# First layer of two tiles in four blocks as seven block products, with planned engine lists

## The chip, the cores and the metric

The kernel runs on one core of one Trainium2 chip. The metric is the device time of one execution in microseconds; before the change the median of three runs is 625.27 us.

## The reference

Input x is 4 x 512 tokens of 256 features. It goes through a gated attention-like layer and then a feed-forward stack, each with a layer normalization before and after and a residual. The change is in the stack, six blocks of:

```python
for i in range(N_BLOCKS):                      # 6
    h = gelu(einsum('bsd,hd->bsh', x, W1[i]) + B1[i])      # 256 -> 1024
    x = einsum('bsh,dh->bsd', h, W2[i]) + B2[i] + x        # 1024 -> 256
    if i < N_BLOCKS - 1:
        x = layernorm(x, LN_G[i], LN_B[i])                 # over the 256 features
```

## The kernel before, in words

A **tile** is one batch of 512 tokens; n = 4 * block + tile numbers the 24 passes of the stack. Features lie on partitions (two chunks k of 128), tokens on the free axis. Every number is held as a high part (fp32r) and a low remainder: XH/XL for activations, WH/WL for weights, HH/HL for the hidden layer. A product of two such numbers is three matmuls (low by high, high by low, high by high), issued by `mm3` (L161 to L167).

A **unit** (n, j) is 128 of the 1024 hidden features of one tile. `mm1` (L326) computes it in 6 matmuls of 512 columns (two chunks of features, three matmuls each) into one of four PSUM banks. ScalarE takes two Gelus from it: `ghi` (L970) writes the high part HH, `gf` (L979) the full value back to PSUM; VectorE's `hlo` (L564) subtracts them to HL. `mm2` (L340) multiplies the unit with the second layer, again 6 matmuls, into the tile's two accumulation banks. From block 1 on TensorE alternates mm1 and mm2, three units apart (L400 to L402, bank order `STEADY`).

After a tile's eight units VectorE adds bias and residual (`y`, L572), and normalizes over partitions: GpSimd adds the chunks (`sum1`, L1249), VectorE transposes and reduces (`tr1`, `red1`), the result goes to DRAM (`put1`, L1343) and comes back to all partitions in four transfers (`got1`, L1347), VectorE totals (`tot1`) and spreads it by a transpose (`mub`), and centres (`ctr`). The same again for the squares: `sqr` (ScalarE), `sum2` (GpSimd), `tr2`, `red2`, `put2`, `got2`, `tot2`, `vae`, then `rsd` (GpSimd, L1259, a power of -0.5), `rsb` and `nn` (L637). `xhi` (ScalarE, L993) and `xlo` (VectorE, L645) split the result for the next block.

Weights of a block come in four pieces p through a staging buffer STG of two halves (`ldp`, L1334), are rounded by ScalarE (`wp_hi`, L843) and their remainder is taken by GpSimd (`wp_lo`, L1169). `kv` (L514) belongs to the attention part.

Each engine works through a list in order. For the attention part and blocks 0 to early 1 the lists are written out call by call (L378 to L399, L712 to L748, L1047 to L1076, L1285 to L1296, L1399 to L1425); then loops follow (L400, L749, L1077, L1297, L1426); the last block's end is written out again. Between engines there are only semaphores, so an instruction late on one engine holds all behind it in that list.

## Time and profile before

| | |
|---|---|
| median of 3 runs | 625.27 us (625.22 to 625.55) |
| the profiled execution | 625.31 us, its span 623.5 us |
| TensorE, VectorE, ScalarE, GpSimd busy | 99%, 74%, 66%, 40% of the span |
| TensorE's mean granted clock | 0.998 of full speed |
| DMA | 25.13 MB moved, mean 40 GB/s |

The profile comes from one execution. Busy time is the union of an engine's instructions, which can overlap on one engine; "idle before, releaser" is what ended the wait ahead of an instruction. L numbers are lines of the kernel before.

### The profile page before, as it was taken

The page shows a single profiled execution, that of the slowest core. Times are in us where ns is not written, and L with a number is a line of the kernel's source. Part 1 is how long each engine was busy: PE and PEld are TensorE (multiplying, and loading weights), DVE is VectorE, ACT ScalarE, POOL GpSimd, SP SyncE. Part 2 cuts the span into 40 slices and gives each one's busy share as a digit, 9 for nine tenths or more (in the row PEclk, how much of TensorE's full clock was granted, in tenths as well). Part 3 has the DMA queues.
Part 4 walks back from the last instruction along what each step waited for, and adds up shares of the span by engine and source line. Part 5 has one row for each costly group of instructions (what it writes and reads, how often), then busy time and mean ns, then how long its engine had stood idle before and what let it go on. Part 6 is the DMA issues. An engine that isn't in the chain of part 4 may idle for free.

```text
span 623.5 us, 8868 instructions
## 1 busy us (share of the span) xinstructions
PE 617.3 (99%) x2893; PEld 516.5 (83%) x2893; DVE 459.9 (74%) x826; ACT 409.0 (66%) x688; POOL 248.7 (40%) x233
## 2 busy tenths in 40 slices
PE   9999999999999999999999999999999999999996
PEld 7888888888888888888888888888888888888886
DVE  6999758886677778676787667767766867666676
ACT  6999986778756675566566556755656665555554
POOL 6666501537434353334532253442344422301234
PEclk9999999999999999999999999999999999999999
DMA  7210000003111020101200110200111100003544
GB/s 293 69 35 1 2 2 0 4 1 106 36 39 40 7 68 6 37 6 37 58 20 3 39 39 2 72 6 5 37 39 38 38 4 6 5 3 68 94 91 156
DMA packets 55821, 25.13 MB, mean 40 GB/s; under 512 B 46816, under 2 KB 51808, under 8 KB 55776
## 3 DMA queue, kind: packets, MB, share of 16 engines
q1 hardware_dynamic: 53376, 24.05, 15.2%
q10 hardware_dynamic: 2400, 0.52, 0.4%
q8 instruction: 23, 0.38, 0.3%
q14 instruction: 22, 0.18, 0.1%
HBM read 20.03 MB, written 4.52 MB: 39 GB/s over the span
## 4 chain that ended last, share of the span: by engine, by line
PE 95%; DVE 1%; DMA 1%; POOL 1%; ACT 0%; issue 0%; ACTq 0%; SPq 0%
PE BK L166 47%; PE BK L356 40%; PE BK L306 4%; PE BK L267 1%; PE BK L270 1%; PE BK L268 1%; PE BK L240 1%; PE BK L260 0%; PE BK L252 0%; PE BK L251 0%; DMA X<-in_x 0%; PE BK L230 0%; DVE R L709 0%; DMA turns<-TB 0%; DMA R<-turns 0%; DVE ST L675 0%
## 5 line engine op out<-in xcount | busy, mean ns | idle before, releaser
L976 ACT ACTIVATE HH<-BK,SM 128x512 fp32r<-128x512 f32 x192 | 132.1, 689 | 153.3 <-PE BK L166 148.3
L569 DVE TENSOR_TENSOR HL<-BK,HH 128x512 fp32r<-128x512 f32 x192 | 131.2, 685 | 84.0 <-ACT BK L982 82.0
L166 PE MATMUL BK<-XH,WL 128*128 128x512 f32 x416 | 162.4, 390 | 0.0
L166 PE MATMUL BK<-XL,WH 128*128 128x512 f32 x416 | 162.1, 390 | 0.0
L166 PE MATMUL BK<-XH,WH 128*128 128x512 f32 x416 | 162.0, 389 | 0.0
L356 PE MATMUL BK<-HH,WL 128*128 128x512 f32 x368 | 143.5, 390 | 0.0
L356 PE MATMUL BK<-HH,WH 128*128 128x512 f32 x368 | 143.2, 389 | 0.0
L356 PE MATMUL BK<-HL,WH 128*128 128x512 f32 x368 | 143.2, 389 | 0.0
L982 ACT ACTIVATE BK<-BK,SM 128x512 f32<-128x512 f32 x192 | 125.2, 655 | 0.0
L166 PEld LDWEIGHTS BK<-XH,WL 128*128 128x128 f32 x416 | 78.1, 188 | 16.6 <-DVE MS L551 0.3
L166 PEld LDWEIGHTS BK<-XH,WH 128*128 128x128 f32 x416 | 78.1, 188 | 16.3
L166 PEld LDWEIGHTS BK<-XL,WH 128*128 128x128 f32 x416 | 78.1, 188 | 15.8
L1263 POOL TENSOR_TENSOR RN<-VN,MH 128x16 f32<-128x16 f32 x20 | 58.7, 2935 | 62.4 <-DVE VN L628 62.4
L356 PEld LDWEIGHTS BK<-HL,WH 128*128 128x128 f32 x368 | 69.1, 188 | 14.3
L356 PEld LDWEIGHTS BK<-HH,WH 128*128 128x128 f32 x368 | 69.1, 188 | 14.3
L356 PEld LDWEIGHTS BK<-HH,WL 128*128 128x128 f32 x368 | 69.1, 188 | 14.2
L1177 POOL TENSOR_TENSOR WL<-STG,WH 128x512 fp32r<-128x512 f32 x48 | 64.5, 1361 | 36.7 <-ACT WH L850 36.6
L1257 POOL TENSOR_TENSOR SA<-SA,TB 128x512 f32<-128x512 f32 x20 | 25.9, 1293 | 127.3 <-ACT TB L991 127.3
L1253 POOL TENSOR_TENSOR SA<-R 128x512 f32<-128x512 f32 x20 | 25.9, 1293 | 39.6 <-DVE R L577 39.6
L1001 ACT ACTIVATE XH<-R,SM 128x512 fp32r<-128x512 f32 x40 | 27.7, 724 | 19.6 <-DVE R L642 19.6
L577 DVE SCALAR_TENSOR_TENSOR R<-BK,SM,R 128x512 f32<-128x512 f32 x46 | 33.5, 731 | 3.4 <-PE BK L356 3.4
L642 DVE SCALAR_TENSOR_TENSOR R<-R,SM,MB 128x512 f32<-128x512 f32 x40 | 35.5, 922 | 0.5
(165 smaller groups left out, 790.1 us busy)
## 6 DMA issues: line engine op xcount, KB each, us to landing
STG<-in_w SPq DMA_DIRECT2D x24, 512.0 KB, 3.8
G<-sums SPq DMA_DIRECT2D x160, 8.0 KB, 1.7
out<-R SPq DMA_DIRECT2D x16, 128.0 KB, 2.0
X<-in_x SPq DMA_DIRECT2D x3, 512.0 KB, 7.7
R<-turns SPq DMA_DIRECT2D x3, 512.0 KB, 4.1
turns<-SA SPq DMA_DIRECT2D x12, 64.0 KB, 2.0
sums<-P SPq DMA_DIRECT2D x40, 8.0 KB, 1.4
R<-in_wv SPq DMA_DIRECT2D x1, 512.0 KB, 5.4
```

The costliest lines, as they stand in the source:

```text
L166: r = eng.matmul(dst, s, m, start=i == 0, stop=i == len(todo) - 1)
L356: r = eng.matmul(acc_of(n)[k][:, :], w, h[:, hs, :], start=(j == 0 and i == 0), stop=(j == 7 and i == 2))
L569: eng.tensor_tensor(HL[:, g % HR, :], bank["mm1", n, j][:, :], HH[:, g % HR, :].bitcast(f32), ALU.subtract).then_inc(S["hlo"], 1)
L577: eng.scalar_tensor_tensor(feat(t, k), by_chunk(acc_of(n)[k][:, :]), BS[:, 2 * b + k:2 * b + k + 1], feat(t, k), ALU.add, ALU.add).then_in ...
L642: eng.scalar_tensor_tensor(feat(t, k), feat(t, k), LG[:, 2 * b + k:2 * b + k + 1], by_chunk(MB[:, 1, :]), ALU.mult, ALU.mult).then_inc(S[" ...
L976: eng.activation(HH[:, g % HR, :], bank["mm1", n, j][:, :], ACT.Gelu, bias=B1[:, 8 * (n // 4) + j:8 * (n // 4) + j + 1]).then_inc(S["ghi"], 1)
L982: eng.activation(ps[:, :], ps[:, :], ACT.Gelu, bias=B1[:, 8 * (n // 4) + j:8 * (n // 4) + j + 1]).then_inc(S["gf"], 1)
L1001: eng.activation(by_chunk(XH[:, F_SLOT[t], k, :]), feat(t, k), ACT.Identity, bias=LB[:, 2 * b + k:2 * b + k + 1]).then_inc(S["xhi"], 1)
L1177: eng.tensor_tensor(WL[:, b % 2, a:a + 512], STG[:, p % 2, 512 * h:512 * h + 512], WH[:, b % 2, a:a + 512].bitcast(f32), ALU.subtract).the ...
L1253: eng.tensor_tensor(by_chunk(SA[:, :]), feat(n % 4, 0), feat(n % 4, 1), ALU.add).then_inc(S["sum1"], 1)
L1257: eng.tensor_tensor(SA[:, :], SA[:, :], TB[:, :], ALU.add).then_inc(S["sum2"], 1)
L1263: eng.tensor_tensor(RN[:, :], VN[:, :], MH[:, :], ALU.pow).then_inc(S["rsd"], 1)
```

## The change

In blocks 1 to 4 (`PAIRED`) tiles 0 and 1 go through the first layer together. The weight (1024 x 256) and the activations of the pair (256 x two tiles) are taken as two-by-two blocks, and the four block results come from seven block products (Strassen's scheme in the form with four sums on each side) in place of eight. Per quarter q of 128 features in each half of the hidden layer there are seven products of three matmuls (`prod1` to `prod7`), for the units (4b, q), (4b, q+4), (4b+1, q), (4b+1, q+4). Two results are copied by ScalarE (`bcopy`, PSUM to PSUM; `tcopy`, PSUM to KB) and added by VectorE (`dsum`, `esum`). The four sums of weights are made by GpSimd (`sadd`, remainder `slo`; ScalarE `shi`), those of activations by VectorE (`tsum`, remainder `tlo`; ScalarE `thi`); three activation blocks are used as they are (`bhi`, `blo`, in place of `xhi`, `xlo`). The second layer is as before. The sums of the normalization are fetched by one transfer instead of four, and may be one tile further ahead. The lists of all engines from block 0's end to block 4 are written out anew, by a planner in which a VectorE instruction and a GpSimd instruction may lock each other out. Some semaphores are merged. Attention and block 5 stay. The core of the diff:

```diff
+PAIRED = (1, 2, 3, 4)
...
+def paired(n):
+    return n // 4 in PAIRED and n % 4 < 2
+
+
+def place(n, j):
+    if not paired(n):
+        return 8 * n + j
+    return 32 * (n // 4) + 4 * (j % 4) + ((1, 2) if n % 4 == 0 else (0, 3))[j // 4]
...
+        def s_weights(i, q):
+            return ((UH, OH)[i // 2][:, i % 2, 128 * q:128 * q + 128], (UL, OL)[i // 2][:, i % 2, 128 * q:128 * q + 128])
...
+            def product(dst, s, m, first, last):
+                for i, (w, v) in enumerate(((s[1], m[0]), (s[0], m[1]), (s[0], m[0]))):
+                    r = eng.matmul(dst[:, :], w, v, start=first and i == 0, stop=last and i == 2, skip_group_check=True)
+                return r
+
+            def prod1(b, q, a, c, d, e):
+                claim(a)
+                pe.wait_ge(S["plo"], 7 * (b - 1) + 3)
+                pe.wait_ge(S["wp_lo"], 8 * b + 4)
+                bank["pair", b, q] = BK[a], BK[c], BK[d], BK[e]
+                bank["before", b, q] = freed[c], freed[d], freed[e]
+                for x, (n, j) in ((a, (4 * b + 1, q)), (d, (4 * b, q)), (e, (4 * b, q + 4)), (c, (4 * b + 1, q + 4))):
+                    bank["mm1", n, j] = BK[x]
+                    freed[x] = S["hlo"], place(n, j) + 1
+                product(BK[a], w_ffn(b, 128 * q, 128), home(B11), True, True).then_inc(S["prod"], 1)
+
+            def prod2(b, q):
+                pe.wait_ge(S["plo"], 7 * (b - 1) + 6)
+                pe.wait_ge(S["pcopy"], 8 * (b - 1) + 2 * q + 1)
+                product(bank["pair", b, q][0], w_ffn(b, 1024 + 128 * q, 128), home(B21), False, True).then_inc(S["mm1"], 1)
+
+            def prod3(b, q):
+                pe.wait_ge(S["plo"], 7 * (b - 1) + 1)
+                pe.wait_ge(S["slo"], 4 * b)
+                pe.wait_ge(S["padd"], 8 * (b - 1) + 2 * q + 1)
+                product(bank["pair", b, q][2], s_weights(3, q), home(B22), False, True).then_inc(S["mm1"], 1)
+
+            def prod4(b, q):
+                pe.wait_ge(S["plo"], 7 * b)
+                pe.wait_ge(S["padd"], 8 * (b - 1) + 2 * q + 2)
+                product(bank["pair", b, q][1], w_ffn(b, 1536 + 128 * q, 128), t_home(b, 3), False, True).then_inc(S["mm1"], 1)
+
+            def prod5(b, q):
+                before = bank["before", b, q][2]
+                pe.wait_ge(*before)
+                pe.wait_ge(S["plo"], 7 * (b - 1) + 4)
+                pe.wait_ge(S["slo"], 4 * b - 3)
+                product(bank["pair", b, q][3], s_weights(0, q), t_home(b, 1), True, True).then_inc(S["prod"], 1)
+
+            def prod6(b, q):
+                pe.wait_ge(S["plo"], 7 * (b - 1) + 5)
+                pe.wait_ge(S["slo"], 4 * b - 2)
+                pe.wait_ge(S["pcopy"], 8 * (b - 1) + 2 * q + 1)
+                product(bank["pair", b, q][1], s_weights(1, q), t_home(b, 2), False, True).then_inc(S["prod"], 1)
+
+            def prod7(b, q):
+                pe.wait_ge(S["plo"], 7 * (b - 1) + 2)
+                pe.wait_ge(S["slo"], 4 * b - 1)
+                pe.wait_ge(S["padd"], 8 * (b - 1) + 2 * q + 1)
+                product(bank["pair", b, q][1], s_weights(2, q), t_home(b, 0), False, True).then_inc(S["mm1"], 1)
...
-            for g in range(8 * 4, 8 * (4 * NB - 1)):
-                mm1(g // 8, g % 8, STEADY[g % 4])
-                mm2((g - LAG) // 8, (g - LAG) % 8)
+            for b in range(1, NB):
+                if b in PAIRED:
+                    a, e, c, d = STEADY
+                    for q in range(4):
+                        g = 32 * b + 4 * q
+                        mm2(*unit(g - 3))
+                        prod1(b, q, a, c, d, e)
+                        prod5(b, q)
+                        mm2(*unit(g - 2))
+                        prod2(b, q)
+                        prod6(b, q)
+                        mm2(*unit(g - 1))
+                        prod3(b, q)
+                        prod7(b, q)
+                        mm2(*unit(g))
+                        prod4(b, q)
+                        e, c, d = d, e, c
+                first_g = 32 * b + (16 if b in PAIRED else 0)
+                for g in range(first_g, min(32 * b + 32, 8 * (4 * NB - 1))):
+                    mm1(*unit(g), STEADY[g % 4])
+                    if b not in PAIRED or g > first_g + 2:
+                        mm2(*unit(g - LAG))
+                    elif g == first_g:
+                        for back in (3, 2, 1):
+                            mm2(*unit(g - back))
...
+            def tsum(b, i):
+                n, p = 4 * b - 4, 2 * (b - 1)
...
+                else:
...
+                ve.wait_ge(S["nn"], 2 * n + (2, 3, 3, 4)[i])
...
+                dst, bias = by_chunk(QB[:, i, :]), LB[:, p + 1:p + 2]
+                if i == 0:
...
+                    r = eng.scalar_tensor_tensor(dst, feat(0, 1), DL[:, b - 1:b], feat(0, 0), ALU.add, ALU.subtract)
+                elif i == 1:
+                    r = eng.tensor_tensor(dst, feat(0, 0), feat(1, 0), ALU.subtract)
+                elif i == 2:
+                    r = eng.scalar_tensor_tensor(dst, feat(0, 1), bias, by_chunk(QB[:, 1, :]), ALU.add, ALU.subtract)
+                else:
+                    r = eng.scalar_tensor_tensor(dst, feat(1, 1), bias, by_chunk(QB[:, 2, :]), ALU.add, ALU.subtract)
+                r.then_inc(S["tsum"], 1)
...
+            def blo(b, i):
+                t, k = ((0, 1), (1, 0), (1, 1))[i]
+                hi, lo = b_home(i)
+                ve.wait_ge(S["phi"], 7 * (b - 1) + (1, 3, 6)[i])
+                eng.scalar_tensor_tensor(by_chunk(lo), feat(t, k), LB[:, 2 * (b - 1) + k:2 * (b - 1) + k + 1],
+                                         by_chunk(hi.bitcast(f32)), ALU.add, ALU.subtract).then_inc(S["plo"], 1)
+
+            def tlo(b, i):
+                hi, lo = t_home(b, i)
+                ve.wait_ge(S["phi"], 7 * (b - 1) + (2, 4, 5, 7)[i])
+                eng.tensor_tensor(lo, QB[:, i, :], hi.bitcast(f32), ALU.subtract).then_inc(S["plo"], 1)
+
+            def dsum(b, q):
+                _, c, d, _ = bank["pair", b, q]
+                ve.wait_ge(S["prod"], 12 * (b - 1) + 3 * q + 3)
+                ve.wait_ge(S["pcopy"], 8 * (b - 1) + 2 * q + 2)
+                ve.wait_ge(*bank["before", b, q][1])
+                eng.tensor_tensor(d[:, :], c[:, :], KB[:, q % 2, :], ALU.add).then_inc(S["padd"], 1)
+
+            def esum(b, q):
+                _, c, _, e = bank["pair", b, q]
+                ve.wait_ge(S["mm1"], place(4 * b, q + 4) + 1)
+                ve.wait_ge(S["pcopy"], 8 * (b - 1) + 2 * q + 2)
+                eng.tensor_tensor(e[:, :], c[:, :], KB[:, q % 2, :], ALU.add).then_inc(S["padd"], 1)
...
+            nn(1, 0); tr1(2); hlo(3, 4); tsum(1, 1); blo(1, 1); hlo(3, 5); tlo(1, 1); tsum(1, 2); hlo(3, 6)
+            nn(1, 1); hlo(3, 7); tlo(1, 2); blo(1, 2); tsum(1, 3); red1(2); tlo(1, 3); dsum(1, 0); hlo(5, 0)
...
+            tr2(8); red2(8); hlo(11, 0); tr2(9); red2(9); hlo(11, 1); tot2(8); vae(8); hlo(11, 2); y(10, 0)
+            y(10, 1); rsb(8); tot2(9); nn(8, 0); hlo(11, 3); vae(9); nn(8, 1); tr1(10); tsum(3, 0); hlo(11, 4)
+            blo(3, 0); tlo(3, 0); rsb(9); hlo(11, 5); nn(9, 0); nn(9, 1); tsum(3, 1); blo(3, 1); hlo(11, 6)
+            tsum(3, 2); tlo(3, 1); tsum(3, 3); hlo(11, 7); tlo(3, 2); blo(3, 2); tlo(3, 3); red1(10); dsum(3, 0)
+            hlo(13, 0); y(11, 0); y(11, 1); tot1(10); esum(3, 0); mub(10); hlo(12, 0); ctr(10, 0); hlo(12, 4)
+            ctr(10, 1); hlo(13, 4); tr2(10); dsum(3, 1); red2(10); hlo(13, 1); tr1(11); esum(3, 1); hlo(12, 1)
...
+            def bhi(b, i):
+                t, k = ((0, 1), (1, 0), (1, 1))[i]
...
+                eng.activation(by_chunk(b_home(i)[0]), feat(t, k), ACT.Identity,
+                               bias=LB[:, 2 * (b - 1) + k:2 * (b - 1) + k + 1]).then_inc(S["phi"], 1)
+
+            def thi(b, i):
+                ac.wait_ge(S["tsum"], 4 * (b - 1) + i + 1)
...
+                eng.activation(t_home(b, i)[0], QB[:, i, :], ACT.Copy).then_inc(S["phi"], 1)
+
+            def shi(b, h):
+                ac.wait_ge(S["sadd"], 4 * (b - 1) + 2 * h + 2)
...
+                eng.activation((UH, OH)[h][:, :, :], SB[:, 2 * h:2 * h + 2, :], ACT.Copy).then_inc(S["shi"], 1)
+
+            def bcopy(b, q):
+                a, c, _, _ = bank["pair", b, q]
+                ac.wait_ge(S["prod"], 12 * (b - 1) + 3 * q + 1)
+                ac.wait_ge(*bank["before", b, q][0])
+                eng.activation(c[:, :], a[:, :], ACT.Copy).then_inc(S["pcopy"], 1)
+
+            def tcopy(b, q):
+                i = 4 * (b - 1) + q
+                ac.wait_ge(S["prod"], 3 * i + 2)
+                if i > 1:
+                    ac.wait_ge(S["padd"], 2 * i - 2)
...
+                eng.activation(KB[:, q % 2, :], bank["pair", b, q][3][:, :], ACT.Copy).then_inc(S["pcopy"], 1)
...
+            gf(11, 3); ghi(11, 4); gf(11, 4); bhi(3, 0); thi(3, 0); ghi(11, 5); gf(11, 5); ghi(11, 6); bhi(3, 1)
+            gf(11, 6); thi(3, 1); ghi(11, 7); gf(11, 7); thi(3, 2); bhi(3, 2); thi(3, 3); bcopy(3, 0); tcopy(3, 0)
+            ghi(13, 0); gf(13, 0); wp_hi(17); ghi(12, 0); gf(12, 0); wp_hi(18); ghi(12, 4); gf(12, 4); ghi(13, 4)
...
+            def dl():
...
+                eng.tensor_tensor(DL[:, :], pairs[:, 1, :], pairs[:, 0, :], ALU.subtract).then_inc(S["bias"], 1)
...
+            def sadd(b, i):
...
+                a11, a21 = STG[:, 1, 0:512], STG[:, 1, 512:1024]
+                a12, a22 = STG[:, 0, 0:512], STG[:, 0, 512:1024]
...
+                left, right, op = ((a21, a22, ALU.add), (SB[:, 0, :], a11, ALU.subtract), (a11, a21, ALU.subtract),
+                                   (a12, SB[:, 1, :], ALU.subtract))[i]
+                eng.tensor_tensor(SB[:, i, :], left, right, op).then_inc(S["sadd"], 1)
+
+            def slo(b, i):
+                hi, lo = (UH, OH)[i // 2], (UL, OL)[i // 2]
+                po.wait_ge(S["shi"], 2 * (b - 1) + i // 2 + 1)
+                eng.tensor_tensor(lo[:, i % 2, :], SB[:, i, :], hi[:, i % 2, :].bitcast(f32),
+                                  ALU.subtract).then_inc(S["slo"], 1)
...
+            wp_lo(5, 0); l3_ve(3); l3_ng(3); l3_rs(3); sadd(1, 0); l3_nb(3); sadd(1, 1); rsd(0); slo(1, 0); sum2(1)
+            slo(1, 1); sadd(1, 2); sadd(1, 3); wp_lo(5, 1); slo(1, 2); slo(1, 3); wp_lo(6, 0); wp_lo(6, 1); rsd(1)
+            sum1(2); wp_lo(7, 0); wp_lo(7, 1); wp_lo(8, 0); wp_lo(8, 1); sadd(2, 0); sadd(2, 1); sadd(2, 2)
...
+                if b in PAIRED and i > 1:
+                    sp.wait_ge(S["sadd"], 4 * (b - 1) + i + 1)
...
-                eng.dma_start(SUMS[n, 0], P1[:, n % 2, :]).then_inc(S["put1"], 16)
+                eng.dma_start(SUMS[n, 0].rearrange("q (g b) -> g q b", g=4), P1[:, n % 2, :]).then_inc(S["put1"], 16)
...
-                for h in range(4):
-                    eng.dma_start(G1[32 * h:32 * h + 32, n % 2],
-                                  SUMS[n, 0].rearrange("(g q) b -> q g b", g=4)).then_inc(S["got1"], 16)
...
+                eng.dma_start(G1[:, n % 2].rearrange("p g b -> p (g b)"),
+                              SUMS[n, 0].unsqueeze(0).to_broadcast([4, 32, 64])).then_inc(S[f"got1_{n % 2}"], 16)
...
```

## Rows read from the trace of the kernel before

**Rows 1.** The page's busy times, share of the span and instruction count

```profile
PE 617.3 (99%) x2893; PEld 516.5 (83%) x2893; DVE 459.9 (74%) x826; ACT 409.0 (66%) x688; POOL 248.7 (40%) x233
```

**Rows 2.** All waits of TensorE: who for whom, us, times, longest

```profile
PE BK L172 <- POOL IDLE L1111: 0.9, 1, 0.9
PE BK L196 <- DVE R L449: 0.3, 1, 0.3
PE BK L267 <- DVE UL L489: 0.2, 1, 0.2
```

**Rows 3.** Stretches: window, length, busy (count) of PE PEld DVE ACT POOL

```profile
287.00:374.00 87.00, 87.00 (x386) 72.06 (x385) 63.35 (x101) 53.06 (x85) 32.99 (x20) 1.00 0.12 29
```

**Rows 4.** Timeline of TensorE: start, length, instruction; 87 rows between these

```profile
350.19 0.39 PE L166 MATMUL BK<-XL,WH 128*128 128x512 f32 x1
...
370.13 0.39 PE L166 MATMUL BK<-XH,WH 128*128 128x512 f32 x1
```

**Rows 5.** Groups by line: shape, count, busy us, mean ns, idle before

```profile
L982 ACT ACTIVATE BK<-BK,SM 128x512 f32<-128x512 f32 x192 | 125.2, 655 | 0.0
L1177 POOL TENSOR_TENSOR WL<-STG,WH 128x512 fp32r<-128x512 f32 x48 | 64.5, 1361 | 36.7 <-ACT WH L850 36.6
L1263 POOL TENSOR_TENSOR RN<-VN,MH 128x16 f32<-128x16 f32 x20 | 58.7, 2935 | 62.4 <-DVE VN L628 62.4
L648 DVE SCALAR_TENSOR_TENSOR XL<-R,SM,XH 128x512 fp32r<-128x512 f32 x40 | 33.2, 863 | 3.6 <-ACT XH L1001 3.5
L1001 ACT ACTIVATE XH<-R,SM 128x512 fp32r<-128x512 f32 x40 | 27.7, 724 | 19.6 <-DVE R L642 19.6
L850 ACT ACTIVATE WH<-STG 128x1024 fp32r<-128x1024 f32 x24 | 25.5, 1061 | 4.2 <-DMA STG<-in_w 2.5 <-PE BK L356 1.7
L521 DVE SCALAR_TENSOR_TENSOR BK<-KB,BK 128x512 f32<-128x512 f32 x8 | 5.5, 691 | 2.0 <-ACT KB L942 1.3 <-PE BK L166 0.7
```

**Rows 6.** Timeline of VectorE, three instructions with no wait between

```profile
362.81 0.67 DVE L616 TENSOR_REDUCE P<-TB 128x16 f32<-128x512 f32 x1
363.40 0.74 DVE L577 SCALAR_TENSOR_TENSOR R<-BK,SM,R 128x512 f32<-128x512 f32 x1
364.06 0.68 DVE L569 TENSOR_TENSOR HL<-BK,HH 128x512 fp32r<-128x512 f32 x1
```

**Rows 7.** Timelines of VectorE and SP: one round trip through DRAM

```profile
234.80 0.68 DVE L616 TENSOR_REDUCE P<-TB 128x16 f32<-128x512 f32 x1
...
239.98 0.26 DVE L622 TENSOR_REDUCE VS<-G 128x16 f32<-128x64 f32 x1 [0.41 <-DMA G<-sums]
...
235.50 0.34 SPq L1357 DMA_DIRECT2D sums<-P  x1
236.92 1.75 SPq L1364 DMA_DIRECT2D G<-sums  x4
```

**Rows 8.** Timelines of TensorE, ScalarE, VectorE: a unit from matmul to hlo

```profile
351.09 0.39 PE L166 MATMUL BK<-XH,WH 128*128 128x512 f32 x1
...
351.52 0.69 ACT L976 ACTIVATE HH<-BK,SM 128x512 fp32r<-128x512 f32 x1 [1.48 <-PE BK L166]
...
352.79 0.69 DVE L569 TENSOR_TENSOR HL<-BK,HH 128x512 fp32r<-128x512 f32 x1
```

**Rows 9.** Timelines of TensorE and VectorE where block 1 begins

```profile
178.60 0.39 PE L166 MATMUL BK<-XH,WL 128*128 128x512 f32 x1
...
184.25 1.82 DVE L642 SCALAR_TENSOR_TENSOR R<-R,SM,MB 128x512 f32<-128x512 f32 x1
```

**Rows 10.** Stretches with written-out lists, columns as in rows 3; sum of 20:178

```profile
20.00:40.00 20.00, 20.00 (x120) 17.48 (x119) 19.83 (x41) 18.87 (x35) 12.07 (x13) 1.00 0.17 54
...
sum 158.00, PE 158.00 PEld 134.52 DVE 126.57 ACT 128.37 POOL 75.61; mean PE 79.00 PEld 67.26 DVE 63.28 ACT 64.18 POOL 37.80
```

**Rows 11.** Timelines of VectorE and GpSimd: two xlo alone, two beside wp_lo

```profile
353.43 1.42 DVE L648 SCALAR_TENSOR_TENSOR XL<-R,SM,XH 128x512 fp32r<-128x512 f32 x2
...
376.14 2.97 DVE L648 SCALAR_TENSOR_TENSOR XL<-R,SM,XH 128x512 fp32r<-128x512 f32 x2 [0.90 <-ACT XH L1001]
...
375.57 2.98 POOL L1177 TENSOR_TENSOR WL<-STG,WH 128x512 fp32r<-128x512 f32 x2 [4.03 <-ACT WH L850]
```

516 lines of the change are left out of this document (318 added, 198 removed).

## The prediction

> **What bounds the kernel now.** I read the shares of the page first: TensorE is busy 99% of the span, VectorE 74%, ScalarE 66%, GpSimd 40% [rows 1]. Then the waits of TensorE: three in the whole execution, 1.4 us together [rows 2]. Then the table by stretches: in a full block of four tiles (the row stands for four alike) TensorE is busy 87.00 of 87.00 us at full clock (2.4 GHz), VectorE 63, ScalarE 53, GpSimd 33 [rows 3]. So time falls only if TensorE gets fewer columns to stream, and it rises only if TensorE is made to wait. The pace is read from its timeline: 88 matmuls between the starts at 350.19 and 370.13, 0.2266 us each, although one lasts 0.39 [rows 4]. A block has 32 units of 12, 384 matmuls, and 384 x 0.2266 is the 87.0.
>
> **What is removed.** For tiles 0 and 1 of blocks 1 to 4 the first layer was 16 units of 6 matmuls (96). Now each of four quarters runs seven products of 3 matmuls (21 for 24), so 84: 12 fewer per block, 48 in all. 48 x 0.2266 = 10.9 us. The second layer keeps its 6 per unit. All of it lies on the path, as TensorE has no idle time to absorb it. The execution whose rows I use took 625.31 us (span 623.5), 0.04 over the median of the three runs, 625.27; I work against 625.31. With no new stall: 625.3 - 10.9 = 614.4.
>
> The Trainium skill ("TensorE: Matmul & The Clock Gate", Back-to-back issue gap) gives N/2.4 + 2.5 ns for isolated matmuls, 216 ns at 512 columns; by it the 48 would be worth 10.4 us. The rows say 227 ns, and decide.
>
> **What is added, per block.** *ScalarE:* 4 thi, 3 bhi for 4 xhi, 2 shi of twice the width, 8 copies out of and into PSUM. With 0.66 to 0.72 us for a 512-wide activation and 1.06 for the wide one [rows 5] that is about 15 x 0.66 + 2 x 1.06 - 0.72 = 11 us of busy time: 53 becomes 64 of a block that now takes 84.3 (372 x 0.2266), 76%. Hidden by TensorE; if uncovered it would cost where a Gelu is late, but a Gelu pair takes 1.24 us and TensorE wants one per some 2.5 us.
> *VectorE:* 4 tsum, 4 tlo, 3 blo for 4 xlo, 4 dsum, 4 esum. At 0.69 to 0.86, and most near the lower [rows 5], about 15 x 0.72 = 11 us: 63 becomes 74 of 84.3, 88%. Back to back, though, these instructions start 0.59 to 0.66 us apart while each shows about 0.7 [rows 6], and "busy" already counts the overlap once, so 72 to 74 is the load.
> *GpSimd:* 4 sadd and 4 slo at 1.36, the same shape as wp_lo [rows 5], 10.9 us: 33 becomes 44, 52%.
> *DMA:* each total of the normalization was fetched by four transfers, now by one. Before: red2 starts 234.80 and lasts 0.68, tot2 starts 239.98 after waiting for the transfer; the put is issued at 235.50, the four gets at 236.92 and take 1.75 us to issue, against 0.34 for one transfer [rows 7]. One get should save about 1.75 - 0.34 = 1.4: from 4.5 to 3.1 us. On no path today; it buys slack for the chain below. SP's list changes order with it; its waits on sadd and wp_lo stand ahead of puts, but none that I can find waits longer than one or two GpSimd instructions.
> The renamed semaphores and the dl instruction cost nothing: they hide among GpSimd's idle time; uncovered, dl would be one short instruction of 0.2 us.
>
> **The new joints in a quarter.** TensorE's order, in matmuls: mm2 (0-6), prod1, prod5 (-12), mm2 (-18), prod2, prod6 (-24), mm2 (-30), prod3, prod7 (-36), mm2 (-42), prod4 (-45), so 10.2 us a quarter. A consumer starts about 0.2 us after the last matmul's slot: the unit starting at 351.09 is used at 351.52, and after both Gelus its hlo starts at 352.79, 1.27 later [rows 8]. bcopy has 12 matmuls (2.7 us) and needs 0.2 + 0.66. dsum must lie between the end of prod6 and prod3: 6 matmuls, 1.36 us, against 0.2 + 0.69 (its nearest row is kv, PSUM and SBUF in, PSUM out, 0.69 [rows 5]) + 0.1. Slack 0.37 us, if VectorE is free at that moment. The same for esum, between prod7 and prod4. These 32 sums are the tight joints: a VectorE instruction just begun costs up to 0.3 us. hlo of the unit wanted at once (mm2(g)) has 15 matmuls, 3.4 us, for 0.2 + 1.24 + 0.6 and a dsum: 0.7 or more over.
>
> **The new boundary.** The tiles of a pair end together, and both must be normalized, split and combined before the next block. I count from the end of the second tile's last mm2. TensorE then has 15 units of mm1 and 14 of mm2 before prod1, 29 x 6 = 174 matmuls, 39.4 us; prod5 needs its data at 40.1, prod2 at 42.2. VectorE in that stretch, from esum to the next dsum (231 matmuls, 52.4 us): 60 instructions of 512 columns and 6 short ones, 60 x 0.65 to 60 x 0.73 plus 1.3, 40 to 45 us. It fits. The chain of one tile alone, by its steps: y 1.3, sum1 1.3, transpose and reduction 1.3, DMA 3.1, total and spread 0.9, centring 1.3, squares 1.3, sum2 1.3, transpose and reduction 1.3, DMA 3.1, total 0.5, rsd 2.94 [rows 5], rsb 0.7: 20 us. The two tiles take turns in it, and the lists hold it back further. vae of the second tile stands behind the hlo of unit 3 of tile 3; that unit's mm1 ends at 4.08 + 8 x 2.72 = 25.8, so the hlo can't start before 27.3. So vae about 29, rsd 32, rsb (behind five instructions for the first tile) 33.8, then nn, tsum, blo, tlo packed tight: blo for prod1 at 37.2 (2.2 us early), tlo for prod5 at 39.1 (1.0 early), blo for prod2 at 41.8 (0.4 early). So it is just in time. The first boundary is alike: block 1's first matmul starts at 178.60 today while tile 1's nn runs at 184.25 [rows 9]; it must move up by over 5 us, with eight more GpSimd instructions (10.9 us) ahead of rsd(1), and the hlo of unit 4 of tile 3 queued behind tr1(2), which waits for sum1 behind that rsd. I count 0 to 2 us there.
>
> **What the joints cost.** No trace row has a dsum. Lower end: nothing, and no gain beyond the 48 matmuls, as the clock is at its top. For it speaks the stretch whose lists are already written out instruction by instruction: from 20 to 178 us TensorE is busy 158.00 of 158.00 while VectorE is at 80%, in one stretch of 20 us even at 19.83 [rows 10]. Upper end: 0.15 us at each of 16 quarters and 1 us at each of four boundaries, 6.4 us. I take 0.2 at each boundary and 0.05 at each quarter, 1.6 us, near the low end because the written-out stretch is the nearest row. **Forecast: 614.4 + 1.6 = 616.0.**
>
> **VectorE against GpSimd.** Two xlo take 1.42 us where GpSimd is idle and 2.97 where it runs two wp_lo, which themselves take 2.98 against a mean of 1.36 each [rows 5, 11]: 1.55 us lost for VectorE. An hlo, with one input in PSUM, shows nothing of the kind. tsum 1, tlo and the others with two SBUF inputs are of the first sort, dsum and esum of the second, but they queue behind it. The Trainium skill ("SBUF — State Buffer", Who interferes with whom) calls this an exclusive lock for the whole instruction, taken by whoever starts first, for VectorE instructions with two SBUF inputs; by it, 8 more GpSimd instructions a block speak against the change. The trace agrees, with the 2.97. In the new lists the last stretch before prod1 has no GpSimd work (wp_lo waits for a wp_hi that ScalarE has behind bcopy), so I charge it only in the rivals.
>
> **Rivals.**
> *Boundaries late.* An rsd, or slo ahead of sum1, slips by one locked instruction (1.3 to 1.55 us) on a chain with 0.4 to 1.0 us of slack: about 1.1 us per boundary, 4.4, plus 0.1 at each quarter, 1.6: 614.4 + 6.0 = 620.4. For it: the packed end. Against: the shorter DMA.
> *Slower: locked VectorE at the sums.* At each dsum and esum VectorE is in an instruction stretched by 0.78 us (half of the 1.55); less 0.37 of slack that is 0.41, and 32 x 0.41 = 13 us: 627.5. It decides from 0.34 us of stall per sum (10.9 / 32). Against: only a few of the 32 follow a two-SBUF-input instruction with GpSimd at work.
> *A draw.* Sums late by 0.3 each: 9.6 us, 624.0 and up. The same holds if the matmuls saved only let TensorE reach waits on other engines earlier, that is if the change takes matmuls away but not time. Against: VectorE at 88%, not 100.
>
> **How the numbers follow.** Forecast 0.70, boundaries late 0.20, draw 0.04, slower 0.06. A measurement tells 0.2% (1.25 us) from nothing, so faster is below 624.0: 0.90; same 0.04; slower 0.06. The range runs from 614.2 (no stall, less a little scatter) to 621.0 (6.4 us of joints, and the first rival); beyond lie the other two.
>
> **What would show it.** Right: 48 fewer matmuls, the rest 0.2266 apart; TensorE's waits for VectorE's dsum and esum small; VectorE 72 to 75 us a block; a paired quarter 10.2 us; red to tot near 3.1 us. Wrong: TensorE waits of over 0.3 us at prod3 or prod4 in most quarters, one of 1 us and more at prod1, prod5 or prod2 of a block, or a granted clock that falls.

## The result and the profile after

The changed kernel takes **631.31 us** (median of 4 runs, 629.07 to 632.11) beside 625.31 for the kernel before: the ratio is 1.0091, 95% interval 1.0078 to 1.0103. Forecast were 616.0 and a range up to 621.0. The profiled execution took 631.38. The first lines of its page; L numbers from here on are lines of the changed kernel:

```profile
span 629.5 us, 8835 instructions
...
PE 614.7 (98%) x2845; PEld 506.2 (80%) x2845; DVE 502.3 (80%) x886; ACT 439.1 (70%) x740; POOL 298.6 (47%) x266
...
PE 73%; DVE 12%; DMA 6%; issue 4%; ACT 3%; POOL 1%; SPq 1%; ACTq 0%; DVEq 0%; POOLq 0%
```

Against [rows 1]: 48 matmuls fewer, as said, yet TensorE is busy only 2.6 us less, and the chain of the end now runs through VectorE (12%) and transfers (6%). Block 2 in two stretches, the quarters of products first (columns as in rows 3):

```profile
273.00:316.60 43.60, 41.36 (x176) 32.05 (x174) 35.57 (x54) 30.57 (x50) 21.04 (x13) 1.00 0.17 52
316.60:361.50 44.90, 44.90 (x199) 37.17 (x198) 37.17 (x61) 30.31 (x50) 23.96 (x15) 1.00 0.02 4
```

Together VectorE is busy 72.7 us of 88.5 (forecast 72 to 75), and the second stretch is without a gap. So the loads were right; the waits were not. Those of TensorE and of the totals, and of the queue of transfers (who for whom: us, times, longest; [rows 2] had 1.4 us in all for TensorE):

```profile
DVE MU L731 <- DMA G<-sums: 16.3, 12, 3.7
...
DVE VS L759 <- DMA G<-sums: 7.4, 8, 2.9
...
PE BK L403 <- DVE BK L830: 2.8, 4, 1.2
...
PE BK L302 <- DVE HL L706: 2.1, 1, 2.1
...
PE BK L403 <- DVE BK L836: 2.0, 2, 1.7
...
SPq L1671 <- POOL WL L1480: 76.5, 17, 11.5
```

L830 is dsum, L836 esum, L403 a product, L302 a transpose of the attention's output; L731 and L759 are the totals tot1 and tot2, L1671 is ldp. In the kernel before the totals waited 5.8 and 8.8 us for their transfers, and ldp 23.7 us, four times.

**Where the 17 us went.** Two landmarks on TensorE's timeline: the start of the first product of block 1, and the length of each block's stretch from the start of its first product to the start of the matmul behind its last (174 matmuls). Undisturbed, the first product starts at 178.60 [rows 9] plus six matmuls, 179.96; a stretch takes 174 x 0.2267 = 39.44. The 198 matmuls between two stretches took 44.87 to 44.90 us for 44.88 at all three places: nothing is lost there, and prod1, prod5 and prod2 of blocks 2 to 4 wait for nothing. All is lost before the first product (5.3 us, a clock fall in it) and inside the stretches (3.4, 4.2, 3.0, 1.1). The sum is 17.0, and 631.4 - 614.4 = 17.0. The same for the kernels of this study (from the last product to the end are 140.1 to 140.2 us more; in e1_sp, e3_start, e4_nosum, g1_start and h1_spstart 140.7 to 141.0, with 0.55 to 0.61 of the excess behind TensorE's last matmul, the cause open; f2_old loses another 0.5 between blocks 1 and 2). The landmarks are those of the one profiled execution, which took 633.35 us in e2_tot, 630.96 in f3_start and 627.83 in i1_lists, so differences of under 1 us in one landmark prove little by themselves:

| kernel | first product | block 1 | 2 | 3 | 4 | median (lowest to highest) |
|---|---|---|---|---|---|---|
| undisturbed | 179.96 | 39.44 | 39.44 | 39.44 | 39.44 | |
| changed | 185.27 | 42.87 | 43.59 | 42.44 | 40.57 | 631.31 (629.07 to 632.11) |
| e1_sp | 184.41 | 42.29 | 42.98 | 40.79 | 40.61 | 628.50 (628.47 to 629.81) |
| e2_tot | 185.95 | 43.03 | 44.53 | 41.59 | 41.43 | 632.40 (631.36 to 633.71) |
| e3_start | 186.50 | 42.48 | 43.76 | 42.58 | 40.57 | 632.69 (631.66 to 633.80) |
| e4_nosum | 184.42 | 40.84 | 42.19 | 42.33 | 40.54 | 628.62 (627.73 to 628.93) |
| f2_old | 185.02 | 44.50 | 44.79 | 45.27 | 41.65 | 639.21 (637.23 to 642.39) |
| f3_start | 187.87 | 41.20 | 42.23 | 42.33 | 40.57 | 632.42 (630.96 to 633.65) |
| g1_start | 186.16 | 42.73 | 42.16 | 42.56 | 40.59 | 632.18 (630.92 to 633.79) |
| g3_splock | 185.59 | 43.79 | 46.89 | 40.78 | 40.57 | 634.89 (634.30 to 636.06) |
| h1_spstart | 184.95 | 41.55 | 42.44 | 40.87 | 40.56 | 627.46 (627.00 to 628.08) |
| h2_splock | 184.48 | 44.20 | 41.77 | 40.87 | 40.57 | 628.79 (627.89 to 630.48) |
| i1_lists | 181.97 | 44.66 | 43.14 | 40.80 | 40.58 | 626.97 (626.67 to 628.16) |
| i2_lists_lock | 181.65 | 44.68 | 41.21 | 40.83 | 40.57 | 625.84 (625.53 to 626.40) |
| j1_cut | 181.70 | 41.28 | 40.82 | 40.69 | 40.55 | 622.28 (621.75 to 622.68) |

**Three readings of the changed kernel's timelines** (start, length, instruction, and in brackets the wait and who ended it) point to three different causes. A matmul is shown with 0.39 us at a pace of 0.2267, so a wait shown as 1.06 sets the next start back by 1.22; most expectations, and the text where it follows them (1.22, 1.38, 1.88, 2.03, 0.40, 0.46, 0.82), give the second number. Block 1's first sum, on VectorE, GpSimd and TensorE:

```profile
186.59 1.78 DVE L817 SCALAR_TENSOR_TENSOR XL<-R,SM,XH 128x512 fp32r<-128x512 f32 x1
188.30 1.77 DVE L810 SCALAR_TENSOR_TENSOR QB<-R,SM,QB 128x512 f32<-128x512 f32 x1
...
190.77 1.01 DVE L823 TENSOR_TENSOR XL<-QB,XH 128x512 fp32r<-128x512 f32 x1
191.70 0.69 DVE L830 TENSOR_TENSOR BK<-BK,KB 128x512 f32<-128x512 f32 x1
...
187.90 1.62 POOL L1503 TENSOR_TENSOR SB<-SB,STG 128x512 f32<-128x512 f32 x1
...
192.53 0.47 PE L403 MATMUL BK<-XH,OL 128*128 128x512 f32 x1 [1.06 <-DVE BK L830]
```

blo (L817) and tsum (L810) take 1.78 and 1.77 us for 0.75 beside GpSimd's sums of weights: the **lock**, 2.1 us in two instructions, and dsum is late. In block 3 it is the **queue of transfers**:

```profile
380.94 0.66 DVE L725 TENSOR_REDUCE P<-TB 128x16 f32<-128x512 f32 x1
...
388.14 0.27 DVE L731 TENSOR_REDUCE MU<-G 128x16 f32<-128x64 f32 x1 [3.72 <-DMA G<-sums]
...
381.63 0.54 SPq L1675 DMA_DIRECT2D sums<-P  x1
383.83 0.33 SPq L1671 DMA_DIRECT2D STG<-in_w  x1
384.94 0.53 SPq L1681 DMA_DIRECT2D G<-sums  x1
...
389.80 0.50 PE L403 MATMUL BK<-XH,OL 128*128 128x512 f32 x1 [1.25 <-DVE BK L830]
```

Between put (381.63) and get (384.94) stands a load of weights, which waits for GpSimd and then runs beside the get; the trip takes 6.54 us, VectorE idles 3.72 of it with a dsum queued behind, and TensorE waits. The longest wait of all at a sum, 1.72 us for the esum of block 2's second quarter, takes both: the get runs beside a load (3.24 us to tot1(7)), so the centring ctr(7,0) starts at 292.08 beside wp_lo and takes 1.57 us, with the esum behind it. In g1_start, whose lists differ only at the end of block 0, the same get takes 2.62 us, ctr(7,0) 0.69, and TensorE waits 0.30. And at the end of block 0 it is the **order of VectorE's list**: tot1(1) waits for its transfer, with hlo(2,5) behind it, whose bank the last transposes need:

```profile
152.96 0.26 DVE L731 TENSOR_REDUCE MU<-G 128x16 f32<-128x64 f32 x1 [3.00 <-DMA G<-sums]
...
156.04 1.12 PE L302 MATMUL BK<-ID,R 128*128 128x128 f32 x4 [2.07 <-DVE HL L706]
163.39 0.47 PE L228 MATMUL BK<-XH,WL 128*128 128x512 f32 x1 [1.19 <-DVE XL L637]
...
156.00:160.00 4.00, 3.96 (x14) 3.34 (x15) 3.43 (x4) 2.96 (x6) 4.00 (x4) 0.63 0.00 0
```

The last row is the table of stretches: after the wait the granted clock was 0.63 of 2.4 GHz, so at 1.2 GHz for most of those 4 us, and six matmuls from 156.81 took 2.48 us for 1.36. A wait of 2.07 us stood before it. Such falls matter for the table: the profiled executions of e2_tot and g3_splock have two, those of the changed kernel, e3_start, f2_old, f3_start and h1_spstart one, each worth 1.1 to 1.7 us by the starts of the matmuls in it, and the others none.

### The profile page after: what moved, and what is told of

It is laid out like the page before. It is cut to its first block, busy times and chain, and to the rows that moved or that the text cites. A ratio compares the mean times of both kernels' runs of the same rounds, so it can differ in the third digit from the quotient of the medians.

```text
span 629.5 us, 8835 instructions
## 1 busy us (share of the span) xinstructions
PE 614.7 (98%) x2845; PEld 506.2 (80%) x2845; DVE 502.3 (80%) x886; ACT 439.1 (70%) x740; POOL 298.6 (47%) x266
## 4 chain that ended last, share of the span: by engine, by line
PE 73%; DVE 12%; DMA 6%; issue 4%; ACT 3%; POOL 1%; SPq 1%; ACTq 0%; DVEq 0%; POOLq 0%
PE BK L471 31%; PE BK L228 27%; PE BK L403 9%; DMA G<-sums 2%; PE BK L368 2%; DMA sums<-P 2%; DVE HL L706 2%; DMA R<-in_wk 1%; DVE R L779 1%; DVE R L714 1%; DVE XL L817 1%; PE BK L329 1%; DMA R<-turns 1%; DVE P L725 1%; PE BK L332 1%
## 5 line engine op out<-in xcount | busy, mean ns | idle before, releaser
L706 DVE TENSOR_TENSOR HL<-BK,HH 128x512 fp32r<-128x512 f32 x192 | 129.5, 679 | 42.6 <-ACT BK L1196 41.8
L228 PE MATMUL BK<-XH,WL 128*128 128x512 f32 x288 | 113.2, 393 | 1.2 <-DVE XL L637 1.2
L228 PE MATMUL BK<-XL,WH 128*128 128x512 f32 x288 | 112.6, 391 | 0.0
L228 PE MATMUL BK<-XH,WH 128*128 128x512 f32 x288 | 112.5, 390 | 0.0
L1480 POOL TENSOR_TENSOR WL<-STG,WH 128x512 fp32r<-128x512 f32 x48 | 66.4, 1403 | 37.8 <-ACT WH L1058 37.8
L1588 POOL TENSOR_TENSOR SA<-SA,TB 128x512 f32<-128x512 f32 x20 | 27.2, 1361 | 96.8 <-ACT TB L1207 96.8
L228 PEld LDWEIGHTS BK<-XH,WL 128*128 128x128 f32 x288 | 54.4, 189 | 13.1 <-DVE XL L637 1.6
L228 PEld LDWEIGHTS BK<-XH,WH 128*128 128x128 f32 x288 | 54.3, 189 | 11.6
L228 PEld LDWEIGHTS BK<-XL,WH 128*128 128x128 f32 x288 | 54.4, 189 | 10.8
L1578 POOL TENSOR_TENSOR SB<-SB 128x512 f32<-128x512 f32 x12 | 15.5, 1294 | 33.8 <-ACT SB L1176 33.6
```

The lines of the kernel that those rows point to most:

```text
L228: r = eng.matmul(dst, s, m, start=i == 0, stop=i == len(todo) - 1)
L706: eng.tensor_tensor(HL[:, g % HR, :], bank["mm1", n, j][:, :], HH[:, g % HR, :].bitcast(f32), ALU.subtract).then_inc(S["hlo"], 1)
L1480: eng.tensor_tensor(WL[:, b % 2, a:a + 512], STG[:, p % 2, 512 * h:512 * h + 512], WH[:, b % 2, a:a + 512].bitcast(f32), ALU.subtract).the ...
L1588: eng.tensor_tensor(SA[:, :], SA[:, :], TB[:, :], ALU.add).then_inc(S["sum2"], 1)
```

## The experiments

**The queue of transfers.** e1_sp changes SP's list at three places and nothing else:

```diff
-ldp(13); got1(3); ldp(14)
+got1(3); ldp(13); ldp(14)
-put2(6); ldp(15); put1(7); got2(6); ldp(16); got1(7)
+put2(6); got2(6); put1(7); ldp(15); got1(7); ldp(16)
-ldp(21); put1(11); ldp(22); got1(11)
+put1(11); got1(11); ldp(21); ldp(22)
```

> The changed kernel, with only SP's list altered: the weight loads 13, 15, 21 and 22 stand behind the gets of the normalization instead of ahead of or between put and get. Changed kernel: 631.3 us, its round trip from red1(11) to tot1(11) 6.5 us, from red1(7) to tot1(7) 6.1. Theory A (round trips: a tot waits for its transfer on VectorE, and the sum that TensorE wants stands behind it): that round trip falls to about 4.3, the stall of 1.40 us at the third quarter of block 3 goes, that of 1.88 at block 2 shrinks: 628 to 630. Theory B (VectorE and GpSimd lock each other): no change, 631. Theory C (the end of block 0): no change, 631.

Measured 628.50, ratio 1.0058 (1.0043 to 1.0073). Block 3's wait is gone:

```profile
383.95 0.27 DVE L731 TENSOR_REDUCE MU<-G 128x16 f32<-128x64 f32 x1 [1.49 <-DMA G<-sums]
...
385.26 0.70 DVE L830 TENSOR_TENSOR BK<-BK,KB 128x512 f32<-128x512 f32 x1 [0.30 <-PE BK L403]
```

dsum now waits for TensorE and not the other way round. The three stretches give 0.6 + 0.6 + 1.65 = 2.85 us. (The start is 0.9 earlier, as the clock stayed at 1.00 in this execution after an equal wait of 2.06 us; the longer end takes that back.) The loads still wait 72.4 us in all for GpSimd's rests: what went is that a get stands behind them.

**The form of the round trip.** f1_form puts the change's put and single get into the kernel before; f2_old puts the contiguous put and four gets into the changed kernel.

```diff
-eng.dma_start(SUMS[n, 0], P1[:, n % 2, :])
-for h in range(4):
-    eng.dma_start(G1[32 * h:32 * h + 32, n % 2], SUMS[n, 0].rearrange("(g q) b -> q g b", g=4))
+eng.dma_start(SUMS[n, 0].rearrange("q (g b) -> g q b", g=4), P1[:, n % 2, :])
+eng.dma_start(G1[:, n % 2].rearrange("p g b -> p (g b)"), SUMS[n, 0].unsqueeze(0).to_broadcast([4, 32, 64]))
```

> The kernel before with the change's two transfers alone: the put in the order of features (a 3-dimensional pattern) and one get that reads the same 32 rows four times, in place of a contiguous put and four gets. Theory now (from the trace after): from the put's issue to the get's 1.95 us instead of 1.42, from the get to its reader 2.2 us where nothing else is in transfer and 3.2 to 3.5 beside a load of weights; so the whole trip stays at 4.2 to 6, saves at most 0.3 us where it is alone, and the time is 625.3 within 0.5. Forecast's reason: 3.1 us for the trip instead of 4.5; a saving of 1.4 us that the kernel before hardly needs either, 625.3 or up to 1 us less. The trace tells the two apart, by the time from red2(3)'s end to tot2(3) in the same place as before (5.18 us from start to start there), not the total.

> The changed kernel with the old put and the old four gets. If the new form is no shorter and its fewer issues are worth nothing (theory now), the time is 631.3 within 1. If the old form's put is worth its 0.5 us at the ends of trips on which TensorE waits (tot1(1), tot1(11)), 630.3. If the new form saves 1.4 us a trip, as the forecast had it, the old form costs at each of three places: 633 to 635.

f1_form took 625.51, ratio 1.0003 (0.9994 to 1.0013). The trip of [rows 7], in its new form:

```profile
233.34 0.67 DVE L616 TENSOR_REDUCE P<-TB 128x16 f32<-128x512 f32 x1
...
238.42 0.26 DVE L622 TENSOR_REDUCE VS<-G 128x16 f32<-128x64 f32 x1 [0.32 <-DMA G<-sums]
...
234.04 0.54 SPq L1356 DMA_DIRECT2D sums<-P  x1
235.99 0.53 SPq L1362 DMA_DIRECT2D G<-sums  x1
```

From red2's end to tot2 4.41 us for 4.50: the get's way is 0.63 us shorter (2.43 for 3.06), the put's 0.53 longer (1.95 for 1.42 from issue to the get's issue). Two transfers, of 8 and 32 KB and each near 2 us, are what it consists of. The Trainium skill ("DMA: Bandwidth & Descriptors", Anatomy of one DMA, given there for transfers that GpSimd issues) has a fixed 2.0 us for each, 4.0 for the two; these rows, issued by SP, agree, and it would have ruled out my 3.1. Yet f2_old took **639.21**, ratio 1.0234 (1.0197 to 1.0271): the old form costs 8 us in the new lists, far beyond every expectation. Groups of the totals in f2_old (count, busy and mean, then idle before them):

```profile
L731 DVE TENSOR_REDUCE MU<-G 128x16 f32<-128x64 f32 x20 | 5.3, 264 | 23.2 <-DMA G<-sums 23.1
L759 DVE TENSOR_REDUCE VS<-G 128x16 f32<-128x64 f32 x20 | 5.2, 259 | 17.4 <-DMA G<-sums 17.4
```

VectorE waits 40.6 us for totals, against 23.9 in the changed kernel and 14.7 before. The reason is in the distances. In the kernel before, tot1 of each of the tiles 5 to 17 starts 8.4 to 11.5 us after the end of its red1, so a trip of 4.4 is hidden; in the changed kernel the same thirteen start after 4.2 to 5.0, but for two that are themselves late, at 6.1 and 6.5. The lists leave hardly more than one undisturbed trip. What a single get gives there is room on SP's queue: four gets take 1.73 us to issue for 0.53, and in f2_old the puts of tiles 3, 5, 9 and 11 are issued 0.6 to 1.5 us late (in the changed kernel 0.6 at most), those of 5 and 9 straight behind the four gets of the tile before. Of f2_old's trips on which VectorE waits the mean is 5.2 us and the longest 7.0. How the 8 us divide between the queue and the longer way of four gets no run tells.

**The totals moved behind the sums.** e2_tot, at four places like this one:

```diff
-tot1(11); mub(11); dsum(3, 2); hlo(13, 2)
+dsum(3, 2); hlo(13, 2); tot1(11); mub(11)
```

> The changed kernel, with only VectorE's list altered at four places: tot1 and mub of the pair's last tile stand behind the next dsum or esum and one hlo instead of ahead of them. Theory A: the DMA waits stay, but no sum stands behind them any more, so the stalls of 1.88 (block 2) and 1.40 (block 3) go: 628 us. Theory B: the locked ctr and nn are still there, the stall in block 2 stays at 0.5 to 1: 629.5 to 631. Theory C: 631.

Measured 632.40, ratio 1.0116: block 3 gains 0.85 us, blocks 2 and 4 lose 0.9 each. In block 2 esum no longer waits, but an hlo does, 2.03 us in place of 1.88, behind two centrings that take 3.13 us beside GpSimd, and the clock falls there in this execution, worth 1.6 us, which is more than the block lost. So of the order alone block 2 shows no loss; what holds is that what must not wait for the total must not wait for what follows it either.

**The lists at the end of block 0.** e3_start and f3_start take work of tile 1 (totals, squares) and of weight sums out of the way of the last transposes and the last xlo3. The core of f3_start:

```diff
 VectorE
-tot1(1); mub(1); ctr(1, 0); ctr(1, 1); hlo(2, 5); rsb(0); nn(0, 0); hlo(2, 6); tr2(1); hlo(2, 7); red2(1); xlo3(3, 0); xlo3(3, 1)
+hlo(2, 5); hlo(2, 6); tot1(1); mub(1); ctr(1, 0); ctr(1, 1); xlo3(3, 0); xlo3(3, 1); rsb(0); nn(0, 0); hlo(2, 7); tr2(1); red2(1)
```

> The changed kernel, altered only at the end of block 0, in order of lists: l3_nb ahead of sadd(1,0) on GpSimd; shi(1,0) behind the Gelus of unit (2,5) and xhi3 ahead of those of (2,7) on ScalarE; hlo(2,5) ahead of tot1(1), and xlo3 ahead of hlo(2,7), on VectorE. In the changed kernel the products begin 5.3 us later than the forecast's count of matmuls puts them: a wait of 2.07 us ahead of a transpose for hlo(2,5), seven matmuls at half clock after it, and a wait of 1.19 for xlo3. Theory C (VectorE waits 3.0 us for tot1(1)'s transfer with hlo(2,5) behind it, and the clock falls for it): the products begin 4 us sooner and the clock stays: 627 us. Theories A and B alone: 630 to 631.

> The changed kernel with three lists mended at the end of the first block alone: on VectorE hlo(2,5), hlo(2,6) ahead of tot1(1) and xlo3(3,.) ahead of rsb(0), nn(0,0); on ScalarE ghi, gf (2,6), xn and xhi3 of the last tile ahead of the two squares of tile 1 and of the roundings of the weight sums; on GpSimd the bias product ahead of the first sum. Theory: the waits of 2.07 and 1.19 us before the last tile's transposes and first matmul come from work put behind the round trip of tile 1, and the fall of the clock behind them; first product at 181 to 182 instead of 185.3, total 627.5 to 628.5. Rival (the statistics of tiles 1 and 2 themselves are what is late): the stop moves to the first products (blo(1,.) late), first product not before 184, total over 630.

e3_start 632.69, f3_start 632.42 (1.0114, interval 1.0098 to 1.0130): misses. In e3_start the transposes started 0.29 us late instead of 2.07, but xlo3 then 3.88 us late (163.03), because ScalarE's squares of tile 1 stood ahead. In f3_start the first was down to 0.28, the second gone, and one of 5.27 us came at 171.44 for hlo(3,0), behind blo(1,0), all of it late since GpSimd's sum2(1) stood behind slo(1,0), which waited for a rounding that I had moved down. g1_start mends that:

> The lists of the start again, with the fault of the last try out: there GpSimd's slo(1,0) stood ahead of sum2(1) and waited 4.71 us for ScalarE's shi(1,0), which was behind the squares, and hlo(3,0) stood behind blo(1,0), so that TensorE waited 5.27 us later on (at 171.44). Now sum2(1) goes ahead of slo(1,0), hlo(3,0) ahead of the first sum of tiles, shi(1,1) and bhi(1,0) behind the last tile's first Gelu. Theory (the stop at the end of the first block is made by the order of the lists): first product at 181.5 to 182.5 instead of 185.3 and the clock at its upper level throughout, time 628 to 629. Rival (VectorE's and ScalarE's new work as such makes the operands late): a wait ahead of the first product, which stays at 184 or later, time over 630.

It took 632.18, another miss. TensorE's waits in it:

```profile
169.92 0.50 PE L228 MATMUL BK<-XH,WL 128*128 128x512 f32 x1 [0.99 <-DVE HL L706]
179.28 0.50 PE L471 MATMUL BK<-HH,WL 128*128 128x512 f32 x1 [2.27 <-DVE HL L706]
183.30 0.50 PE L228 MATMUL BK<-XH,WL 128*128 128x512 f32 x1 [0.97 <-DVE HL L706]
```

Over four microseconds in three waits, a little later. The rival "VectorE is full there" got its first support. The table of stretches for 150 to 190, before and changed:

```profile
150.00:190.00 40.00, 40.00 (x182) 33.20 (x182) 27.27 (x45) 26.98 (x44) 19.58 (x14) 1.00 0.16 43
...
150.00:190.00 40.00, 36.33 (x155) 29.03 (x155) 32.96 (x41) 26.75 (x44) 33.91 (x23) 0.96 0.18 55
```

VectorE is busy 5.7 us more with *fewer* instructions (41 for 45, as TensorE gets through 155 matmuls for 182), beside a GpSimd that works 33.9 us instead of 19.6.

**The sums of weights left out.** e4_nosum leaves out sadd, slo and shi of blocks 2 to 4 (block 1's sums are used again, so its output isn't the reference's). With them go six ScalarE instructions and the loads' wait for sadd.

> The changed kernel without the sums of weights of blocks 2, 3 and 4 (sadd, slo and shi left out; those blocks reuse block 1's sums), so 24 fewer GpSimd and 6 fewer ScalarE instructions, TensorE's work the same. Theory B (the lock): the instructions of 1.7 to 1.8 us on VectorE that stand beside sadd at the start of block 1's products (blo 1.78, tsum 1.77) return to 0.7, the stall of 1.22 us there goes; the stalls beside wp_lo stay; 628 to 629.5. Theory A: only what loads of weights stand in the way changes, 630 to 631. Theory C: 631.

Measured 628.62, ratio 1.0052 (1.0037 to 1.0067). Block 1's stretch falls by 2.0 us and block 2's by 1.4. The second is no evidence for the lock, as block 2 falls by the same 1.4 in f3_start and g1_start, where its lists are untouched. The first is: without sadd beside them blo and tsum are short again, and the wait behind them is gone:

```profile
185.74 0.75 DVE L817 SCALAR_TENSOR_TENSOR XL<-R,SM,XH 128x512 fp32r<-128x512 f32 x1
186.40 0.75 DVE L810 SCALAR_TENSOR_TENSOR QB<-R,SM,QB 128x512 f32<-128x512 f32 x1
```

**GpSimd's work moved.** g3_splock and h2_splock, both on e1_sp, put sadd(2,·) behind the first rest of block 2's weights and the rests of parts 15 and 16 a quarter later.

> The order of the transfers of the first experiment (628.5), and in blocks 1 and 2 GpSimd's instructions moved off VectorE's two-input ones: the sums of weights of block 2 behind the first rest of block 2's weights, so about 8 us later, and the rests and roundings of weight parts 15 and 16 one quarter later. Theory (the lock is what makes the first four sums' operands late in block 1 and esum(2,1) late in block 2): the wait of 1.22 us before prod3(1,0) and of 1.38 us before prod4(2,1) go, 0.2 to 0.5 us comes back later in the quarters: 626 to 627. Rival (VectorE's wait for the get, 1.24 us before tot1(7), makes block 2's wait, and the amount of VectorE's work block 1's): less than 0.7 us of change, 628 to 628.5.

> The order of the transfers, and GpSimd's instructions moved off VectorE's two-input ones as in g3_splock, with what came back there repaired. There the two waits aimed at went (1.22 us before prod3 of block 1: gone; 1.38 before prod4 of block 2: 0.40), and new ones of 1.99 and 3.38 came, because sum2(2) stood on GpSimd behind the moved work and put2(7) on the queue of transfers behind two loads that now waited longer. Now sum2(2) and put2(2), put2(7) go first. Theory (lock and order of lists, both mended): stretches of products of block 1 at 41.2 and of block 2 at 41.8 instead of 42.3 and 43.0, time 626.3 to 627. Rival (every place on GpSimd's list is as bad as another, since VectorE is full): 628 or more.

g3_splock 634.89, h2_splock 628.79. In both, the wait of 1.22 us in block 1 goes; block 2's, 1.38 in e1_sp, falls to 0.40 and 0.82 (g1_start has 0.46 there without such a move, so block 2 proves nothing). But in g3_splock put2(7) stood behind two loads that waited for the moved work, and VectorE waited 5.81 us for it at tot2(7):

```profile
313.60 0.26 DVE L759 TENSOR_REDUCE VS<-G 128x16 f32<-128x64 f32 x1 [5.81 <-DMA G<-sums]
...
315.38 0.50 PE L403 MATMUL BK<-XH,OL 128*128 128x512 f32 x1 [3.23 <-DVE BK L830]
```

and in h2_splock ScalarE's rounding of weight part 12 waited 2.56 us for its load ahead of bcopy, and TensorE 2.89 for that bcopy. Both are my lists' faults: queues that I moved work past.

**All of it, place by place.** h1_spstart is e1_sp with a third version of the start's lists; i1_lists mends four more places that h1_spstart's trace names; i2_lists_lock adds block 2's part of h2_splock.

> The order of the transfers and a third version of the lists of the start. In the last one three waits of TensorE came back later, each for a rest hlo of tile 3 (1.16, 2.42, 1.12 us, at 169.9, 179.3, 183.3) that stood on VectorE behind work on the coming block: hlo(3,1) behind blo(1,0), hlo(3,4) behind rsb(1), which waited 1.62 us for GpSimd's power, hlo(3,5) behind a locked sum and blo(1,1). Now each of them stands ahead of it, and on ScalarE the Gelus of (3,1) and (3,5) ahead of bhi and of weight part 8. Theory (TensorE stops there only by the order of the lists): first product at 182 to 183 instead of 184.4, time 626.5 to 627. Rival (VectorE is full from 155 on, with the locked instructions in it, and whatever is put first something else is late): first product at 184 or later, time 628 to 629.

> h1_spstart (627.5) with the four places mended that its trace names: on ScalarE weight part 7, which waited 2.20 us for its load, behind the Gelus of (3,3) and (3,4); on GpSimd the sum of tile 2's halves ahead of the last rest of weight sums, on VectorE its transpose behind the sum of tiles and hlo(3,5) (it waited 1.19 us); and in block 2 esum(2,1) directly behind mub(7), ahead of ctr(7,0) (1.34 us, locked). If order is all that is wrong: first product at 183 instead of 184.95, the 1.02 us wait in block 2 gone, 624.5 to 625.5. If VectorE's load sets it: again a new wait, 627 or more.

> The same, and in block 2 alone GpSimd's rests and ScalarE's roundings of weight parts 15 and 16 one quarter later, with put2(7) and got2(7) ahead of the two loads that then wait longer. In h2_splock this part took block 2's stretch from 43.0 to 41.8 us. Expected 0.3 to 0.7 us below i1_lists; if esum's order already took what the lock cost, the same as i1_lists.

627.46 (1.0034, interval 1.0021 to 1.0047), 626.97 (1.0031) and **625.84** (1.0011, interval 1.0002 to 1.0020; 11 runs): the last is within 0.2% of the kernel before. In its profiled execution the losses are 1.7 us at the start and 5.2, 1.8, 1.4 and 1.1 in the stretches, 11.2 together: they eat the 10.9 us of the 48 matmuls. Four combinations were expected at 623.5 to 625.5, as if the single gains added, and all missed: f4_all (e1_sp's order, f3_start's lists and the old gets) 637.34, g2_spstart (e1_sp and g1_start) 628.73, g4_all (that and g3_splock) 634.83, h3_all (h1_spstart and h2_splock) 630.17. So the gains do not add: g2_spstart is no faster than e1_sp alone (628.50). The table's rows show what holds. From h1_spstart to i1_lists the first product moved up by 3.0 us and block 1's stretch grew by 3.1; its last product starts at 226.3 and 226.4, as in e1_sp (226.5). h1_spstart's execution even has a clock fall of 1.6 us ahead of its first product, and i1_lists none. Order alone does not move that point in these three.

**The lock taken away.** j1_cut is i2_lists_lock with two kinds of GpSimd instruction shortened where VectorE is full, all waits and signals kept. It leaves out most of block 2's weight sums and the low parts of block 1's second-layer weights (it reads those of the first layer in their place, by a line not printed here), so it measures a cause and is no kernel to use:

```diff
 wp_lo
+w = 8 if p in (7, 8) else 512
-eng.tensor_tensor(WL[:, b % 2, a:a + 512], STG[:, p % 2, 512 * h:512 * h + 512], ...)
+eng.tensor_tensor(WL[:, b % 2, a:a + w], STG[:, p % 2, 512 * h:512 * h + w], ...)
 sadd
+w = 8 if b == 2 else 512
-eng.tensor_tensor(SB[:, i, :], left, right, op)
+eng.tensor_tensor(SB[:, i, 0:w], left[:, 0:w], right[:, 0:w], op)
```

> The best version so far (i2_lists_lock) with GpSimd's rests of weight parts 7 and 8 of block 1 and the four weight sums of block 2 cut from 512 to 8 columns each: the order and VectorE's work are the same, what goes is 8 times 1.3 us of GpSimd's reading beside VectorE at the end of block 0 and in the first quarter of block 1. Left out with it: the low parts of the second layer's weights of block 1 (those of the first layer are read in their place) and most of block 2's weight sums. In i2_lists_lock four of VectorE's instructions took 1.67, 1.79, 1.77 and 1.77 us there (176.5 to 184.4) for 0.68 to 0.74 alone, 4.2 us too much, and TensorE waited 0.93, 0.50, 1.50 and 1.03 us behind them, for hlo, for a rest of a sum and for blo. Theory (the lock, not the number of VectorE's instructions, holds block 1): block 1's stretch of products 41 instead of 44.7, time 622 to 623. Rival (the number of instructions holds it): less than 1 us of change, 625 to 625.8.

Measured **622.28**, ratio 0.9954 (0.9937 to 0.9970), 3.6 us below i2_lists_lock. VectorE at the same instructions (blo, tlo, tsum), first in i2_lists_lock:

```profile
179.29 1.79 DVE L817 SCALAR_TENSOR_TENSOR XL<-R,SM,XH 128x512 fp32r<-128x512 f32 x1
181.01 1.77 DVE L823 TENSOR_TENSOR XL<-QB,XH 128x512 fp32r<-128x512 f32 x1
182.70 1.77 DVE L808 SCALAR_TENSOR_TENSOR QB<-R,SM,QB 128x512 f32<-128x512 f32 x1
```

and in j1_cut (one line further down in its file):

```profile
179.34 0.70 DVE L818 SCALAR_TENSOR_TENSOR XL<-R,SM,XH 128x512 fp32r<-128x512 f32 x1
179.96 0.68 DVE L824 TENSOR_TENSOR XL<-QB,XH 128x512 fp32r<-128x512 f32 x1
180.56 0.74 DVE L809 SCALAR_TENSOR_TENSOR QB<-R,SM,QB 128x512 f32<-128x512 f32 x1
```

Block 1's stretch is 41.28 us for 44.68, and of the four waits there only the first (0.77 us) is left. The number of VectorE's instructions is the same, and from 172 to 179.3 its timeline agrees within 0.1 us. So it is the lock that holds the start of block 1 once the lists are in order. Even so 622.28 lies above the stated range: 7.3 us are still lost, 1.7 before the first product, some 2.4 by a slower pace among the products (see the end) and the rest in short waits. The Trainium skill ("SBUF — State Buffer", Who interferes with whom) has it that the engine that issues second blocks for the other's whole instruction; the trace agrees, as the excess of 1.0 to 1.1 us nears GpSimd's 1.3. An order that keeps all the work and avoids it there wasn't found, nor much looked for: in GpSimd's list only the four sadd of the eight instructions were moved, in g3_splock and h2_splock.

## Why the prediction was wrong

Of the 17.0 us that were lost, the edits named above took 9.0 away (631.31 to 622.28), the last 3.6 only by leaving work out. Step by step:

- **Removed work: right,** 2845 matmuls for 2893. **"The rest 0.2266 apart": wrong among the products,** where steps without a visible wait are 0.230 us; this term wasn't in the sum and costs some 2.4 us in the four stretches. Elsewhere the pace is 0.2267.
- **Added load: right.** In block 2 VectorE 72.7 us, ScalarE 60.9 (forecast 64), GpSimd 45.0 (44).
- **"From 4.5 to 3.1 us", the round trip: wrong, the term mis-sized.** It is 4.4 alone (f1_form), since the put with its rearranged pattern gives back what the get saves, and 4.2 to 6.5 in the changed kernel. I took the issue time of four gets for their share of the path. The step behind it, that the transfer "buys slack", was wrong in kind: the lists had spent that slack, and more.
- **SP's waits, "none that I can find waits longer than one or two GpSimd instructions": wrong.** Its loads wait 76.5 us in all, up to 11.5, and in four places one stands ahead of a get that is due. Cost, by e1_sp: 2.8 us. I read the list and did not simulate the queue.
- **The lock, "I charge it only in the rivals": wrong, the main miss.** I looked at the last stretch before prod1 and found it free of GpSimd, which is so (in the 5 us before block 2's first product GpSimd is busy 0.00 and VectorE 5.00), and nothing waits there in blocks 2 to 4. But it isn't in block 0's end, where 14 us more of GpSimd's work lies beside VectorE, nor right behind prod1, where sadd and wp_lo come. Worth 3.6 us by j1_cut, nearly all at one place and in the lists of i2_lists_lock; in the changed kernel's own lists e4_nosum shows 2.0 in block 1. What the lock costs in all no run measures.
- **The first boundary, "0 to 2 us": wrong.** 5.3, of which some 1.1 is the clock; 1.7 in i2_lists_lock, but with 3 us of it only moved into block 1. I counted the chain of tile 1's statistics but not what stands in the lists behind its waits: hlo(2,5) behind tot1(1), xlo3 behind the squares.
- **Boundaries 2 to 4, "just in time": right,** and cheaper than the 0.2 each that I took.
- **The joints, 0.05 a quarter: too low.** Block 4, the calmest, loses 1.1 us in its stretch, 0.28 a quarter; only 0.5 of it are visible waits, most of the rest is the pace.
- **The rivals.** None is what happened. "Locked VectorE at the sums" has the mechanism and the sign, but it priced 32 equal small delays; the trace has three single waits of 1.1 to 1.7 us at sums, 4.0 of the 17.0 us. 0.06 for slower was far too little: there are several causes, each small and each likely, 5.3 us at the start, 2.8 of queue, the lock, the pace, and mending one in part only uncovered the next.

## What to carry over

When lists are planned, look for the instruction that waits longest (here a total behind a trip through DRAM) and ask who is queued behind it on every engine, transfers among them: a plan tight to the undisturbed length turns each disturbance into a stop of the engine that bounds. Before giving GpSimd more work, count it beside VectorE's instructions with two SBUF inputs, stretch by stretch, since a share of 80% can hide stretches of 100%. And a change whose gain is under 2% should be charged for what its new waits may cost one by one, not with the mean of the old kernel.

## What the runs showed of the hardware

- The lock holds small instructions too. vae (L765, 16 columns, a single SBUF input) takes 0.17 us alone and 1.12 beside wp_lo. The same section of the Trainium skill names this kind of instruction (tensor_scalar, in its two-port mode) among those that can contend; the trace agrees, with the 1.12. I had passed over it because it is short:

```profile
145.68 1.12 DVE L765 TENSOR_SCALAR VN<-VS 128x16 f32<-128x16 f32 x1
...
288.69 0.17 DVE L765 TENSOR_SCALAR VN<-VS 128x16 f32<-128x16 f32 x1
```

- TensorE's pace among products is a little slower than elsewhere, with no wait shown. Two starts in block 4 of the changed kernel, with six rows left out between:

```profile
449.27 0.39 PE L403 MATMUL BK<-XH,WH 128*128 128x512 f32 x1
...
450.88 0.40 PE L471 MATMUL BK<-HH,WL 128*128 128x512 f32 x1
```

  Seven steps in 1.61 us, 0.230 each for 0.2267; over the stretch (40.57 less 0.51, the excess of its five steps of over 0.24 us) / 174 = 0.2302, some 0.6 us a block. The cause is open.
- The clock fell after a wait of 2.07 us in the changed kernel's profiled execution and stayed at its top after one of 2.06 at the same place in e1_sp. Over all runs, falls follow waits of 1.85 (h1_spstart) to 5.27 us (f3_start), and none follows waits of 2.22 (e4_nosum), 2.27 (g1_start) and 2.89 us (h2_splock): the length of the one wait before does not decide it. A fall costs 1.1 to 1.7 us.
